# A graph network on one core: the first convolution's selection tables built between the columns of a dense group, one register load for the finished nodes, and a ramp held in PSUM in the other two convolutions

## The reference

```python
def conv(h, W, b):
    m = jnp.concatenate([h[dst], h[src], edge_attr], axis=1) @ W + b
    return jax.ops.segment_sum(m, dst, num_segments=n_nodes)
h = jax.nn.relu(conv(x, W1, b1))
h = jax.nn.relu(conv(h, W2, b2))
return conv(h, W3, b3)
```

## Time and profile before

| | before |
|---|---|
| median of 3 runs | 9293.24 us (9290.43 to 9294.93) |
| the profiled execution, its own time | 9304.37 us |
| its span in the trace | 9302.5 us |
| first convolution, about | 140 to 2210 us |
| second and third convolution, about | 2210 to 4720 us |
| PNA layers with what lies around them | the rest |
| busy share: PE, PEld, DVE, ACT, POOL | 79%, 64%, 48%, 26%, 62% |

### The profile page before, as it was taken

The page is one execution under the profiler, slowest core; times in us unless marked ns, Lnnn a source line. Parts: engine busy times, 40 slices in busy tenths (PEclk is TensorE's granted clock), DMA queues, the critical chain, the costliest instruction groups (busy, mean ns, idle before and its releaser), DMA issues. The chain is left out here.

```text
span 9302.5 us, 178267 instructions
## 1 busy us (share of the span) xinstructions
PE 7322.9 (79%) x56432; PEld 5977.1 (64%) x56433; DVE 4425.5 (48%) x5729; ACT 2397.5 (26%) x3942; POOL 5795.6 (62%) x5901
## 2 busy tenths in 40 slices
PE   2777778776888887888857888888886888887885
PEld 2656656655777776888846666666665666666663
DVE  4655555553111212111126665656664666665665
ACT  2545545452000000000012222222223222222223
POOL 2444444443777756777727777777764777777773
PEclk9988888888888888989968898989897988998897
DMA  4444434435666666666742222222222222222222
GB/s 115 155 153 147 160 141 153 154 141 183 232 230 245 236 206 232 249 249 241 259 108 63 72 68 69 72 69 71 69 67 64 72 69 72 69 68 69 72 72 57
DMA packets 562586, 1230.78 MB, mean 132 GB/s; under 512 B 311863, under 2 KB 391838, under 8 KB 533328
## 3 DMA queue, kind: packets, MB, share of 16 engines
q1 hardware_dynamic: 362120, 748.77, 23.3%
q0 software_dynamic: 187232, 233.06, 12.2%
q10 hardware_dynamic: 13160, 248.05, 6.6%
HBM read 948.01 MB, written 281.42 MB: 132 GB/s over the span
## 5 line engine op out<-in xcount | busy, mean ns | idle before, releaser
L842 POOL DMA_INDIRECT data<-h_parts,idx x2508 | 2595.2, 1035 | 2070.2 <-issue 1039.1
L1726 POOL DMA_INDIRECT data<-q_rows,idx x3328 | 3151.6, 947 | 1156.3 <-issue 1001.9
L963 PE MATMUL p_z<-hs,adj 128*128 128x192 bf16 x22638 | 2275.9, 262 | 290.6 <-DMA adj<-counted 157.1
L963 PEld LDWEIGHTS p_z<-hs,adj 128*128 128x128 bf16 x22638 | 2078.8, 105 | 595.2 <-issue 402.1
L1058 ACT CAST adj<-p_count 128x1012 bf16<-128x1012 f32 x836 | 911.3, 1100 | 605.9 <-PE p_count L952 597.8
L1928 DVE TENSOR_TENSOR_SCAN run<-reset,run,p_turn 128x1024 f32<-128x1024 bf16 x416 | 974.2, 2342 | 151.7 <-PE p_turn L1793 147.1
L1858 ACT COPY back<-p_back 128x1024 f32<-128x1024 f32 x418 | 423.2, 1012 | 2413.0 <-PE p_back L1746 2413.0
L555 DVE TENSOR_TENSOR hot<-p_ramp,ends 128x2048 f32<-128x2048 f32 x416 | 949.7, 2283 | 0.5 <-issue 0.4
L1752 PE MATMUL part<-hot,t 128*128 128x128 f32 x6688 | 913.1, 296 | 45.2 <-issue 45.2
L1752 PEld LDWEIGHTS part<-hot,t 128*128 128x128 f32 x6688 | 882.0, 213 | 45.7 <-issue 45.7
L1757 PE MATMUL part<-hot,back 128*128 128x128 f32 x6688 | 815.1, 275 | 0.0
(11 more groups left out here) (300 smaller groups left out, 6724.4 us busy)
## 6 DMA issues: line engine op xcount, KB each, us to landing
adj<-counted SPq DMA_DIRECT2D x152, 3136.0 KB
counted<-adj ACTq DMA_DIRECT2D x76, 3136.0 KB
reset<-flags SPq DMA_DIRECT2D x208, 512.0 KB
data<-q_rows,idx POOLq DMA_INDIRECT x3328
data<-h_parts,idx POOLq DMA_INDIRECT x2508
feat<-in_ea_blocks SPq DMA_DIRECT2D x208, 128.0 KB
ea<-in_ea_cols SPq DMA_DIRECT2D x154, 88.0 KB
rden<-node_rows SPq DMA_DIRECT2D x50, 256.0 KB
```

The costliest lines, as they stand in the source:

```text
L842: pool.indirect_dma_start(out=data[:, p, j, 0:PARTS], out_offset=None, in_=table[:, :], in_offset=bass.IndirectOffsetOnAxis(ap=idx[:, p, j ...
L963: mm = pe.matmul(p_z[:, 0:PARTS], adj[:, (q + 1) % 2, hi, :], hs[:, hi, :], start=(hi == 0), stop=(hi == BLOCKS - 1))
L1726: pool.indirect_dma_start(out=data[:, r, j, :], out_offset=None, in_=q_rows[:, :], in_offset=bass.IndirectOffsetOnAxis(ap=idx[:, r, j:j + ...
```

## The change

Four edits.

1. **Tables between columns** (first convolution only). DVE no longer prepares tables in P positions or ahead of column 2. In each E group at position n it splits the attributes for group n + 1 behind column 3 and builds that table behind column 4, and does the same for group n + 2 behind columns 7 and 8. The prologue builds one table instead of two.
2. **One load.** `chip.quads` holds both bounds of a turn in one word (next bound times 32 plus this one). An engine loads it once and takes it apart by two register operations. The same is done for the PNA layers (`chip.nodes`).
3. **The load moved ahead.** On PE it stands behind the products of the last P group, ahead of `scatter`; on DVE it stands, with the base for `finish`, ahead of `finish_dense`.
4. **Ramp in PSUM** (convolutions 2 and 3). The comparison that builds `hot` takes its ramp from `p_end`, a PSUM bank that is not used there, filled once by ACT; it was the SBUF tile `ramp16`.

```diff
-def finished_quads(chip, eng, k, body, ready=None, table=None):
-    table = chip.quads if table is None else table
-    bound = lambda at: eng.value_load(table[0:1, bass.ds(at, 1)], min_val=0, max_val=QUADS)
-    low, high = bound(k + 1), bound(k + 2)
+def quads_of(eng, table, k):
+    both = eng.value_load(table[0:1, bass.ds(k + 1, 1)], min_val=0, max_val=(QUAD_BASE + 1) * QUADS)
+    low = eng.snap((both & (QUAD_BASE - 1)).with_bounds(min_val=0, max_val=QUADS))
+    return low, eng.snap((both >> 5).with_bounds(min_val=0, max_val=QUADS))
+
+def finished_quads(eng, bounds, body, ready=None):
+    low, high = bounds
     with eng.If(high > low):
...
             with pe.Fori(0, KT) as k:
                     if pos in POS_P:
                         by_window(k, pos, POS_P.index(pos))
+                        if pos == POS_P[-1]:
+                            finished = quads_of(pe, chip.quads, k - 1)
                         for q in done_with(pos):
                             scatter(k, q, k * H + (nth[pos] + 1))
...
                         if pos == POS_P[-1]:
                             turn(k, pos)
-                            finished_quads(chip, pe, k - 1, convolve, banks_read)
+                            finished_quads(pe, finished, convolve, banks_read)
...
         @block.scalar
         def _(act):
+            if not first:
+                nc.scalar.copy(p_end[:, 0:P], chip.ramp[:, :]).then_inc(s_ramp, 1)
...
             def build_hot(k, n):
-                return v.tensor_tensor(hot[:, n % 2], chip.ramp16[:, :].unsqueeze(1).broadcast_to([P, GC, P]),
+                ramp = chip.ramp16[:, :] if first else p_end[:, 0:P]
+                return v.tensor_tensor(hot[:, n % 2], ramp.unsqueeze(1).broadcast_to([P, GC, P]),
...
-            for n in (0, 1):
+            if not first:
+                v.wait_ge(s_ramp, 1)
+            for n in range(1 if first else 2):
                 prepare_hot(0, n, False)
...
+                        if pos == POS_P[-1]:
+                            begin = begin_of(k, pos)
+                            finished = quads_of(v, chip.quads, k - 1)
                         for q in done_with(pos):
                             finish_dense(k, q, k * H + (nth[pos] + 1))
                         if pos == POS_P[-1]:
-                            finish(k, pos)
-                            nodes(k)
-                        prepare_hot(k, nth[pos] + 2)
+                            finish(k, pos, begin)
+                            nodes(finished)
+                        if not first:
+                            prepare_hot(k, nth[pos] + 2)
                     else:
                         q = POS_E.index(pos)
                         if first:
-                            prepare_hot(k, nth[pos] + 2)
                             for i in range(2, GC):
                                 pair(k, q, i)
                                 if i == 2 and pos - 1 in POS_P:
                                     finish(k, pos - 1)
+                                if i in (3, 7):
+                                    table_free(k, nth[pos] + (1 if i == 3 else 2))
+                                    split_ea(k, nth[pos] + (1 if i == 3 else 2))
+                                if i in (4, 8):
+                                    build_hot(k, nth[pos] + (1 if i == 4 else 2)).then_inc(s_hot, 1)
```

More of the change, by code:

```diff
@@ L39 @@
 QUADS = NP // P // QUAD
+QUAD_BASE = 32
+assert QUADS < QUAD_BASE
 HB = QUADS * QUAD
@@ L240, in prepare @@
         pna_ends = sb("pna_ends", [P, NG + 1, 2 * G], I16)
-        pna_quads = sb("pna_quads", [1, TURNS + 2], I32)
+        pna_quads = sb("pna_quads", [1, TURNS + 1], I32)
+        bounds = sb("bounds", [1, 2, TURNS + 2], I32)
         pna_regs = sb("pna_regs", [1, 3, NG + 1], I32)
@@ L453, in _, with pack @@
             then(v.tensor_scalar(chip.slots[:, 1:], chip.slots[:, 1:], slot_w[:, 0:1], None, ALU.add))
-            v.memset(chip.quads[:, 0:2], 0)
-            v.tensor_scalar(chip.quads[:, 2:KT + 1], base[:, TURN::TURN], 9, None,
-                            ALU.arith_shift_right)
-            v.memset(chip.quads[:, KT + 1:], QUADS)
+            def pack(to, first_nodes, n, turns):
+                v.memset(bounds[:, n, 0:2], 0)
+                v.memset(bounds[:, n, turns + 1:turns + 2], QUADS)
+                then(v.tensor_scalar(bounds[:, n, 2:turns + 1], first_nodes, 9, None, ALU.arith_shift_right))
+                then(v.scalar_tensor_tensor(out=to[:, :], in0=bounds[:, n, 1:turns + 2], scalar=float(QUAD_BASE),
+                                            in1=bounds[:, n, 0:turns + 1], op0=ALU.mult, op1=ALU.add))
+            pack(chip.quads, base[:, TURN::TURN], 0, KT)
             v.wait_ge(s_counts, 64)
@@ L496, in _ @@
             then(v.tensor_scalar(span[:, 1, :], span[:, 0, :], 7, None, ALU.arith_shift_right))
-            v.memset(pna_quads[:, 0:2], 0)
-            v.tensor_scalar(pna_quads[:, 2:TURNS + 1], rows[:, 0, SLOTS::SLOTS], 9, None, ALU.arith_shift_right)
-            v.memset(pna_quads[:, TURNS + 1:], QUADS)
+            pack(pna_quads, rows[:, 0, SLOTS::SLOTS], 1, TURNS)
             v.memset(wf[:, 0, 0:1], 1.0)
@@ L820, in _ @@
                     if pos == POS_P[-1]:
-                        finished_quads(chip, sp, k - 1, store)
-            finished_quads(chip, sp, KT - 1, store)
+                        finished_quads(sp, quads_of(sp, chip.quads, k - 1), store)
+            finished_quads(sp, quads_of(sp, chip.quads, KT - 1), store)
             sp.wait_ge(s_out, 32 + 16 * QUADS)
@@ L1036, in _ @@
             gate(pe)
-            finished_quads(chip, pe, KT - 1, convolve)
+            finished_quads(pe, quads_of(pe, chip.quads, KT - 1), convolve)
         @block.scalar
         def _(act):
+            if not first:
+                nc.scalar.copy(p_end[:, 0:P], chip.ramp[:, :]).then_inc(s_ramp, 1)
             for p, pos in enumerate(POS_P):
@@ L1110, in summed @@
                     act.wait_ge(s_dense_added, k * NQ + 2)
-                finished_quads(chip, act, k - 1, stage, summed)
+                finished_quads(act, quads_of(act, chip.quads, k - 1), stage, summed)
             further_windows_of(act, further)
@@ L1171, in split_ea, with table_free @@
                 split_in_three(ea[:, b], to, s_ea_step, k * (4 * TURN) + 4 * n)
+            def table_free(k, n):
+                v.wait_ge(s_part, k * H + (H + n - 1))
             def prepare_hot(k, n, begun=True):
                 if begun:
-                    v.wait_ge(s_part, k * H + (H + n - 1))
+                    table_free(k, n)
                 if first:
@@ L1183, in window, with begin_of, finish @@
                 return bass.ds(at, P)
-            def finish(k, pos):
+            def begin_of(k, pos):
+                return v.value_load(chip.cregs[0:1, BASE, bass.ds(k * TURN + (pos + 1), 1)], min_val=0, max_val=N)
+            def finish(k, pos, base=None):
                 n = nth[pos]
-                base = v.value_load(chip.cregs[0:1, BASE, bass.ds(k * TURN + (pos + 1), 1)], min_val=0, max_val=N)
+                base = begin_of(k, pos) if base is None else base
                 rows, at = (slice(0, M), M) if pos in POS_P else (slice(D, KC), EA)
@@ L1311, in rows, with nodes @@
                 v.tensor_tensor(part(2), conv[:, :, :], part(1), ALU.subtract).then_inc(s_h, 1)
-            def nodes(k):
-                finished_quads(chip, v, k - 1, rows)
+            def nodes(finished):
+                finished_quads(v, finished, rows)
                 v.memset(scratch[:, 1:2], 0.0).then_inc(s_nodes, 1)
@@ L1372, in _ @@
             finish_dense(KT, 0, KT * H + 1)
-            nodes(KT)
+            nodes(quads_of(v, chip.quads, KT - 1))
 def pipeline(eng, *stages):
@@ L1667, in nodes @@
         def nodes(eng, k, body, ready=None):
-            finished_quads(chip, eng, k - 1, body, ready, chip.nodes)
+            finished_quads(eng, quads_of(eng, chip.nodes, k - 1), body, ready)
         at_nodes = lambda n: bass.ds(n * CH, CH)
@@ L2130, in __init__ @@
         self.ends = held("kept_ends", [P, NG + 1, 2 * G], I16)
-        self.quads = held("kept_quads", [1, TURNS + 2], I32)
+        self.quads = held("kept_quads", [1, TURNS + 1], I32)
         self.regs = held("kept_regs", [1, 3, NG + 1], I32)
@@ L2174, in gnn @@
             chip.rare = sb("rare", [1, 3], I32)
-            chip.quads = sb("quads", [1, KT + 2], I32)
+            chip.quads = sb("quads", [1, KT + 1], I32)
             prepare(chip, x_pad, src_cols, dst_pad, dst_cols, heads, col_ends, col_heads, firsts, slot_heads, flags,
```

3 lines of the change are left out of this document (2 added, 1 removed).

## The result

The changed kernel takes 8794.77 us (median of 4 runs, 8791.53 to 8798.88), against 9294.08 for the kernel before (4 runs); the ratio is 0.9463 with an interval of 0.9447 to 0.948. The forecast was 8964 with a range from 8865 to 9115: right in direction, and 169 us short of the gain. The profiled execution took 8792.25 us, 512 less than the one of before.

A forecast was written before the change was run, and what follows sets the result against it. It took chained waits (PE for high_hot, then adj) to bound the convolutions and POOL's gathers the PNA layers. 168 + 55 + 57 + 46 + 3 = 329 us off 9304.4 gives 8975, less 11.1 is 8964; range 8865 to 9115.

The forecast's parts named there:

- A: First convolution: tables built between columns remove most of PE's stalls for high_hot; 168 us, bounds 85 and 273.
- B: End of a first-convolution turn: PE's gap shrinks as its load is issued during the products; 55 us, bounds 25 and 75.
- C: First convolution: behind the shorter end-of-turn gap PE's clock stays up or recovers earlier; 57 us, bounds 0 and 85.
- D: Convolutions 2 and 3: shorter PE gaps, earlier convolve, and gathers freed of the table build; 46 us, bounds 15 and 110.
- E: Prologue: one table less to build, 3 us; the ramp's copy is hidden by the load of hs.
- I take 1.4 us a group: First convolution, each E group: the stall left at column 9, about 0.9 us plus 0.5 for slower high_hot beside a gather.
- crowded columns: Rival, chance 0.2: DVE has too little room between columns, 2.4 us a group remain; gain 194 us, time 9099.
- through the wait of 2.68 us it stays at 1.00: Second E group of a first-convolution turn: PE's granted clock holds 2.4 GHz through its high_hot wait.
- one slow step and a little, 1.2 us: First-convolution turns behind a quad: clock recovers during columns 0 and 1, saving 1.2 us 22 times, 26 us.
- The rule that I had weighed against C: Rival, chance 0.04: repeated short waits drop PE to 1.2 GHz in E groups; slower, up to 9773 us.
- more: Rival, chance 0.12: the clock also holds in convolve and little stall remains; gain 428 us, time 8865.

The follow-up runs named there:

- b_tables2: The kernel before with only the tables between columns in the first convolution, on a usual chip: 8960.83 us, ratio 0.9648.
- a_together: The changed kernel with split and table build in one piece behind columns 4 and 8, no column between them: 8889.07 us, ratio 0.9564.
- a_dve_early: The changed kernel with DVE's three end-of-turn loads moved ahead of the last evacuation in the first convolution: 8765.87 us, ratio 0.9438.
- b_ramp2: The kernel before with only the table build's ramp in PSUM in convolutions 2 and 3, on a usual chip: 9263.76 us, ratio 0.9971.
- b_oneload2: The kernel before with only the two loads made one, in the old places, on a usual chip: 9219.11 us, ratio 0.9924.
- a_bring: The changed kernel with SP asking for the next turn's adj ahead of storing the finished rows in convolutions 2 and 3: 8663.54 us, ratio 0.9325.
- a_idle_mid: The changed kernel with two idle PE register loads ahead of column 2 of the first convolution's second dense group, on a slow chip: ratio 0.9986.

## Why the prediction was wrong

The forecast was too small by 183 us on the profiled execution (8975 against 8792). By its own terms:

| term | forecast | measured | how |
|---|---|---|---|
| A, stalls for `high_hot` | 168 | 272 (259 in the steady loop) | 315.9 - 44.0 |
| B, end of the turn | 55 | 43 | 314.4 of idle time less 272 |
| C, clock, first convolution | 57 | 101 | PE busy |
| D, convolutions 2 and 3 | 46 | 101 (82 against `b_tables2`) | stage |
| E, prologue; PNA layers | 3; 0 | 0; -4 | stage |

**A was mis-sized.** The mechanism and the places were right: what remains stands at column 9. But the step "I take 1.4 us a group" added up three things that did not come. It had PE at column 9 after 11.7 us where it came after 12.7; it added 0.5 us because `high_hot` grows beside a gather, and the mean was 506 ns, 526 before (I had gone by the one of 0.68 us); and it took each overrun for a wait. The outer bound, 273 if nothing remains, was the right end, with 12.5 us of the 272 from the first and the last wait, which the forecast had left out. The rival "crowded columns" (2.4 us a group) is refuted by 0.25; its mechanism is real when an insertion is 3 us long (`a_together`).

**C failed in its step on where the clock falls.** The forecast gave both slow steps of the earlier trace rows to the gap of 2.87 us, and nothing to the stalls of turns without a quad. `b_tables2` shows otherwise: with that gap in place and the stalls gone, columns 2 and 3 run at full clock. And "through the wait of 2.68 us it stays at 1.00" was read from one turn, and counted for all. The turn before has a wait of the same 2.68 us with the clock at 0.50 behind it, and so have 9 of 33. Behind the 22 waits of over 4 us I counted "one slow step and a little, 1.2 us". It was two steps: the 5.36 us from 965.87 to 971.23 are one of the longer cases, and the mean of the 22 is 4.74 us where full clock has 2.85, so 1.9 us each, 42 in all. Column by column, PE's busy time in the first convolution fell like this:

| columns | forecast | measured |
|---|---|---|
| 2 and 3 of the first dense group, behind the first stall | 26 + 20 | 66 |
| 2 and 3 of the second, behind the stall of 2.68 us | 0 | 14 |
| 0 and 1, behind the end of the turn | 11 | 19 |
| last column, with the end of the turn | 0 | 15 |
| all others | 0 | -13 |

The 20 and the 11 are the forecast's 2.1 us a turn, 15 times, parted by column. So 80 of the 101 us stand right behind the stalls for `high_hot`. The edits taken singly fit: 60 us came with edit 1 alone, 26 with edits 2 and 3 alone. What made the last column shorter and the others longer was not looked into.

The rule that I had weighed against C, in the Trainium skill's "TensorE: Matmul & The Clock Gate", section "A second HAM failure mode: psum-queue depth-cycling", did not come true for the changed kernel: its short waits (1.1 us at most in a group in the steady loop) left the clock at 0.95. In the kernel before, whose waits were longer (2.3 to 6.6 us), the clock did swing between 0.50 and 1.00, which my reading did not have.

**B was about right**, 43 for 55. PE's waits behind the turn and ahead of `convolve` fell by 34 us each, as forecast. Of the difference, 6 us are DVE's later `acc`: I had put it at 0.3 us a turn, and PE's wait for it grew by 0.5 (0.6 to 1.1), which `a_dve_early` takes back. Another 6 are waits for evacuated columns (`adj`, 8.0 to 14.3), which the forecast did not have.

**D was mis-sized.** Of its parts, the gap of the turn gave 36 us (133.4 to 97.6) for 26, the one ahead of `convolve` 18 for 15, and the gathers 26 by `b_ramp2`, for 5. (PE's waits for them fell by 6 only, 27.1 to 20.8, but with the loads alone they rose to 52.5.) The clock in `convolve` was put at nothing and stood only in the upper bound of 110; PE busy fell by 40 us. There PE now waits 0.79 us in place of 1.15 ahead of `convolve`:

```profile
2408.18 1.67 PE L996 MATMUL p_z<-identb,hs 128*64 128x128 bf16 x12 [0.79 <-DVE acc L1214]
2409.83 1.08 PE L1002 MATMUL p_part<-wsum,sums 113*128 113x65 f32 x8
```

The same eight matmuls took 1.88 us at 3039.94 of the kernel before, at a clock of 0.50. Over both convolutions 23 of the 52 such runs take over 1.3 us, where it was 37, and their median is 1.08 for 1.78. `b_oneload2` has it too (1.09), `b_ramp2` does not (1.54), so it goes with the loads. That the shorter wait alone keeps the clock up is not shown, and `a_bring` speaks against it: it has the same waits of 0.8 us, and the median is 1.56. So the cause of D's 40 us of busy time stays open.

Right were the direction, the place of the remaining wait, that the waits for `adj` would stay (157.1 and 153.7) as part of the chain through the finished rows, which `a_bring` shows, and the PNA layers. The rival "more" (0.12, 8865) had the mechanism that came: little stall left and the clock up in `convolve`. It was given too little, and even its sum was 70 us short, since it left A at 205.

## What to carry to other kernels

Work for a later group can be put between the steps of an engine that is waited for, as long as each piece is no longer than what the buffers ahead cover; if a piece is twice as long, the waits come back under several names. A wait of some microseconds on TensorE can cost more than its length, because the matmuls behind it run at half clock (all 22 waits of over 4 us here, 9 of 33 of 2.7 us): price a stall with the time of the steps behind it, and count those steps in many turns before taking one turn as typical. And two waits in series hide one another: the end of the turn alone was worth 71 us in the first convolution, and 90 once the tables were out of the way.

## What was unexpected of the hardware

**Chips differ.** The kernel before took 9290 us on some chips and 13486, 13207 and 13199 us on three others. It is not one engine: in `a_idle_mid` ACT and DVE stand still together, released by nothing that this core's trace shows. ACT, then DVE:

```profile
1206.77 3.67 ACT L1075 CAST adj<-p_count 128x1012 bf16<-128x1012 f32 x3 [8.64 <-remote]
```

```profile
1206.78 0.51 DVE L1246 TENSOR_SCALAR high_hot<-iota,code 128x1078 f16<-128x1078 f16 x1 [8.13 <-remote]
```

The cause was not found. It matters for judging an edit: tables between columns gave 3.5% on the usual chip and 0.5% on such a one, and the ramp in PSUM gave 0.3% on the one and cost 1.9% on the other.

**A register load is short or long by its place, and the gap that it leaves is another matter.** On PE's sequencer the load of `quads` took 0.92 us behind the `turn` and 0.30 us in every turn of the changed kernel, where it stands behind the products. The two idle loads ahead of column 2 in `a_idle_mid` took 0.90 us each, and still PE stood still for 1.3 us only, where two loads with their register work at the end of a turn left 2.87. In the turn of 502.03 shown above the first of them began at 498.66, while PE worked on what had been issued ahead of it until 500.71. What makes the load itself three times as long was not found out.
